# Moving the points at which three token-sum buffers change hands, are folded, loaded and stored

## The chip, the cores and the metric

One core of a Trainium2 chip runs the whole program. The metric is device time in microseconds (us). Shorter names: PE is the matrix engine, DVE the vector engine, ACT the scalar engine, POOL the engine that issues the indirect transfers, SP the engine that issues most of the plain transfers. A transfer moves over 16 DMA engines, whichever engine issued it.

## The reference

Sixteen images of 128 channels and 28x28 pixels pass a convolution block, and their 12544 pixels, as tokens, then pass a mixture of eight experts in which each expert picks its 1024 best tokens. The change touches only how the experts' outputs are added up and written back:

```python
logits = x_flat @ Wr
probs = jax.nn.softmax(logits, axis=0)
vals, idx = jax.lax.top_k(probs.T, C)          # C = 1024 tokens for each of 8 experts
selected = x_flat[idx]
h = jax.nn.gelu(jnp.einsum('ecd,edf->ecf', selected, W1) + b1[:, None, :], approximate=False)
out_e = jnp.einsum('ecf,efd->ecd', h, W2) + b2[:, None, :]
weighted = vals[..., None] * out_e
output = jnp.zeros_like(x_flat).at[idx.reshape(-1)].add(weighted.reshape(-1, Dd))
...
t = t + ffn(layernorm(t));  x = from_tokens(t)  # back to channels by pixels
```

## The kernel before

Everything is ordered by hand: each engine has one program, and semaphores tie them. Experts are numbered 0 to 7 in the code. The convolution and the choice of tokens come first; the experts begin near 240 us and the change lies from 320 us on.

**One expert** on PE is `hidden` for two halves of 512 tokens (4 matmuls each, L936), the turning of the next expert's picked tokens (`turn_picked`, L907), and `down` for two halves (32 matmuls each listed as 16 pairs, L948). ACT does the gelu. DVE adds the bias (`bias_out`, L1437) and multiplies by the gate (`weigh`, L1445) into one of two buffers `y_rows[e % 2]`, so `weigh` of expert e waits until the scatter of expert e - 2 has landed. POOL gathers the tokens of the experts to come in blocks of 128 (`gather`, L472, 8 blocks for an expert) and scatters an expert's result into a sum in DRAM, 8 blocks for an expert. The last expert, `last_expert`, does its two halves one behind the other, so that its first half is scattered while the second is computed.

**Three sum buffers** in DRAM, `moe_sum`, `moe_sum_mid` and `moe_sum_late`, take turns: `FIRST_OF_SUMS` lists the expert that opens each. The opening expert's scatter writes plainly (L495), the others add (L498; L492 for the last expert). An adding scatter waits until the scatter before it has landed, a writing one does not.

**A fold** takes one image of a finished sum: SP loads it as token rows (`load_sums`, L384), PE turns it to channel rows with 7 transposes (`turn_sums`, L978), DVE adds it in two parts to `x1_all` (`add_sums`, L1452). `moe_sum` is folded behind experts 3, 4 and 5 (`FOLDS_BEHIND`), `moe_sum_mid` around the last expert's second half (`MID_FOLDS` ahead of it, the others after). SP issues the loads of a sum once its scatters have landed. PE waits at the end of each group for DVE's folds, since the fold uses PSUM that the next expert needs.

**The end.** `moe_sum_late` is loaded image by image as the last expert's blocks land: `load_late` waits for the turning of that image's middle sum and for as many landed blocks as a number in `need` says, which SP reads from memory. ACT counts landed blocks. PE turns the image (L1033), DVE adds it to `x1_all` into one of four buffers `o_img` (L1521), and the image is stored. SP stores images 0 to 7, in turn with its loads of images 8 to 15, ACT stores images 8 to 15.

```python
for img in range(B):
    load_late(img)
    if img >= B - STORED_BY_SP:
        stored = img - (B - STORED_BY_SP)
        sp.wait_ge(s_fa, stored + 1)
        sp.dma_start(out_d[:, ds(stored, 1), :], o_img[stored % ENDS]).then_inc(...)
```

## Time and profile before

| | us |
|---|---|
| median of 3 runs (470.76 to 477.99) | 471.27 |
| the profiled execution's own time | 471.32 |
| its span in the trace | 469.5 |
| the last expert's last block, issue to landing | 435.26 to 441.40 |
| first output store issued | 440.40 |

Time of day in the trace counts from the span's start; the profiled execution spent 1.8 us outside the span and stands 0.05 us above the median, so a difference of spans is taken as a difference of times. A row of the timeline gives start, duration, engine, line, what is written from what, how many instructions were merged, and in brackets how long the engine sat idle before it and what released it.

### The profile page before, as it was taken

What the parts mean: (1) busy time and instruction counts of PE and PEld (TensorE: products, weight loads), DVE (VectorE), ACT (ScalarE), POOL (GpSimd) and SP (SyncE); (2) the same over time, 40 slices, a digit from 0 to 9 for tenths busy, and PEclk for the clock granted to TensorE, in tenths of its full rate; (3) what the DMA queues carried; (4) which work ended last, traced back from release to release, by engine and by line L of the source; (5) the groups of instructions that cost most, each with busy time, mean ns of one, the idle gap of its engine ahead of it and who ended that gap; (6) DMA issues with size and microseconds to landing.
All of it is one profiled execution on the core that took longest, in us unless ns stands there. A gap on an engine that the chain in (4) does not pass through costs nothing. (4 is left out here: it accounts for less than half of the span.)

```text
span 469.5 us, 8092 instructions
## 1 busy us (share of the span) xinstructions
PE 359.3 (77%) x2577; PEld 249.3 (53%) x2577; DVE 329.2 (70%) x1086; ACT 257.1 (55%) x528; POOL 157.2 (33%) x152
## 2 busy tenths in 40 slices
PE   2778998999999879301148799996998989778752
PEld 2435655666556657200113568766484847637642
DVE  3478788898999886788887697776486342335744
ACT  3469898899998873566701665752343433520000
POOL 4000000000000000010037777787778887766100
PEclk9989999999999995555555999998799989979955
DMA  4456577767676644899902232357986449969897
GB/s 110 128 143 194 159 237 255 227 225 229 201 240 235 194 147 140 261 390 328 320 23 54 54 100 78 76 80 165 296 240 124 86 41 267 290 111 216 260 370 292
DMA packets 42323, 89.07 MB, mean 190 GB/s; under 512 B 7568, under 2 KB 18992, under 8 KB 42288
## 3 DMA queue, kind: packets, MB, share of 16 engines
q1 hardware_dynamic: 32224, 76.62, 51.3%
q0 software_dynamic: 8576, 8.72, 11.0%
q10 hardware_dynamic: 1488, 3.30, 1.8%
q8 instruction: 18, 0.29, 0.3%
q14 instruction: 17, 0.14, 0.1%
HBM read 41.45 MB, written 36.81 MB: 167 GB/s over the span
## 5 line engine op out<-in xcount | busy, mean ns | idle before, releaser
L776 PE MATMUL psC<-x_pad,tap_diag 64*64 64x392 f32 x384 | 68.2, 501 | 8.9 <-issue 5.1
L776 PE MATMUL psC<-hid,tap_turned 64*64 64x392 f32 x384 | 68.2, 501 | 0.0
L503 POOL TENSOR_TENSOR logits_T<-top,logits_T 112x896 f32<-112x896 f32 x1 | 1.7, 1682 | 197.7 <-ACT top L660 197.7
L948 PE MATMUL psC<-w,hid 128*128 128x128 f32 x448 | 52.8, 277 | 1.8 <-ACT hid L702 1.7
L948 PEld LDWEIGHTS psC<-w,hid 128*128 128x128 f32 x448 | 51.0, 192 | 3.9 <-ACT hid L702 3.0
L702 ACT ACTIVATE hid<-psB,b_T 128x512 f32<-128x512 f32 x32 | 21.9, 687 | 53.9 <-PE psB L936 53.9
L776 PEld LDWEIGHTS psC<-x_pad,tap_diag 64*64 64x64 f32 x384 | 28.0, 135 | 37.6 <-issue 28.7
L472 POOL DMA_INDIRECT picked<-token_rows,slot_idx x32 | 31.3, 979 | 45.7 <-issue 44.8
L936 PE MATMUL psB<-picked_T,w 128*128 128x512 f32 x64 | 37.6, 719 | 6.5 <-DVE x_all L1452 3.3
L580 ACT ACTIVATE ln_tok<-psA,sm 112x128 f32<-112x128 f32 x112 | 40.9, 477 | 0.9 <-DVE sm L1089 0.9
L1437 DVE TENSOR_TENSOR y_sum<-psC,b_rows 128x512 f32<-128x512 f32 x14 | 9.6, 688 | 39.3 <-PE psC L948 39.3
L1097 DVE SCALAR_TENSOR_TENSOR work<-x_pad,taps_w,work 128x784 f32<-128x784 f32 x32 | 33.1, 1035 | 1.1
L806 PE MATMUL psB<-work,pw_masked 128*128 128x392 f32 x64 | 26.5, 539 | 5.3 <-DVE pw_masked L1203 2.7
L936 PE MATMUL psC<-picked_T,w 128*128 128x512 f32 x64 | 30.5, 599 | 0.0
L873 PE MATMUL psA<-sign_sum,half_same 128*128 128x4 f16 x16 | 3.0, 187 | 35.2 <-ACT x_in L640 34.2
L1097 DVE SCALAR_TENSOR_TENSOR work<-x_pad,taps_w,psC 128x392 f32<-128x392 f32 x32 | 18.5, 619 | 14.4 <-PE psC L776 14.4
L1046 DVE BATCH_NORM_STATS2 st<-psA 112x6 f32<-112x128 f32 x112 | 23.7, 282 | 7.0 <-PE psA L815 6.9
L603 ACT ACTIVATE work<-psB,fold 128x392 f32<-128x392 f32 x32 | 21.0, 678 | 12.3 <-PE psB L806 12.3
L672 ACT ACTIVATE picked_T<-psA 128x512 f32<-128x512 f32 x16 | 8.8, 594 | 33.0 <-PE psA L907 33.0
L498 POOL DMA_INDIRECT moe_sum_mid<-y_rows,slot_idx x16 | 25.1, 1568 | 4.9 <-issue 4.9
L776 PEld LDWEIGHTS psC<-hid,tap_turned 64*64 64x64 f32 x384 | 25.8, 135 | 0.0
L1293 DVE TENSOR_SCALAR_CACHE_REDUCE work<-dist,cand 128x784 bf16<-128x784 f32 (+1 forms) x31 | 24.6, 829 | 1.1 <-DVE cand L1311 0.7
(280 smaller groups left out, 873.3 us busy)
## 6 DMA issues: line engine op xcount, KB each, us to landing
token_rows<-rows SPq DMA_DIRECT2D x16, 422.6 KB, 4.9
x_in<-in_x_dram SPq DMA_DIRECT2D x16, 392.0 KB, 3.4
x_res<-in_x_dram SPq DMA_DIRECT2D x16, 392.0 KB, 4.0
moe_sum<-hid SPq DMA_DIRECT2D x16, 392.0 KB, 4.5
x_all<-work SPq DMA_DIRECT2D x16, 392.0 KB, 3.0
moe_sum_mid<-hid SPq DMA_DIRECT2D x16, 392.0 KB, 5.7
moe_sum_late<-hid SPq DMA_DIRECT2D x16, 392.0 KB, 4.8
w<-in_L_ffn_W_dram SPq DMA_DIRECT2D x16, 256.0 KB, 3.1
```

The source lines that it names most:

```text
L472: nc.gpsimd.indirect_dma_start(out=picked_in[k][:, b, :], out_offset=None, in_=rows_dram, in_offset=bass.IndirectOffsetOnAxis(ap=slot_idx[ ...
L498: nc.gpsimd.indirect_dma_start(out=sums, out_offset=at, in_=y_rows[:, q, b, :], in_offset=None, compute_op=ALU.add).then_inc(s_sca[q], 16)
L580: ins = nc.scalar.activation(ln_tok[:, q1, t * C:(t + 1) * C], ln_tiles[:, t, :], ACT.Identity, bias=ln_sm[:, 6, t:t + 1], scale=ln_sm[:, ...
L603: nc.scalar.activation(act2[:, q3, h * HALF:(h + 1) * HALF], psB[:, h, 0:HALF], ACT.Relu, bias=fold[:, 9:10], scale=fold[:, 5:6]).then_inc ...
L702: nc.scalar.activation(hid[:, f, h * HS:(h + 1) * HS], hidden_bank[f], ACT.Gelu, bias=b1_T[:, ds(e * FT + f, 1)]).then_inc(s_gelu, 1)
L776: ins = nc.tensor.matmul(psC[col * HC:col * HC + HC, half, 0:HALF].rearrange("c (h w) -> c h w", w=W), weights[of, n, :], lines[of, q, dy: ...
L806: nc.tensor.matmul(psB[:, h, 0:HALF], pw_masked[:, q, :], act1[:, q, h * HALF:(h + 1) * HALF], start=True, stop=True).then_inc(s_pw, 1)
L936: nc.tensor.matmul(hidden_bank[f], w1[:, q, f * 128:(f + 1) * 128], picked_T[:, h * HS:(h + 1) * HS], start=True, stop=True).then_inc(s_l1, 1)
L948: ins = nc.tensor.matmul((psA if first else psC)[:, h, b * C:(b + 1) * C], hid[:, f, lo:lo + 128], w2[:, q, f * C:(f + 1) * C], start=(f = ...
L1046: ins = nc.vector.bn_stats(st[:, t, :], ln_tiles[:, t, :])
L1097: return nc.vector.scalar_tensor_tensor(o, x_pad_v[:, q, y0 + dy:y0 + dy + lines, dx:dx + W], taps_w[:, PE_TAPS + n:PE_TAPS + n + 1], acc, ...
L1293: return nc.vector.tensor_scalar(junk[:, column, 0:n], dist[:, 0:n], value.bitcast(F32), -offset, ALU.is_lt, ALU.add, accum_out=cnt[:, col ...
```

## The change

The sums are cut at experts 0 to 2, 3 to 5 and 6 to 7, where they were cut at 0 to 1, 2 to 4 and 5 to 7. The first is folded behind experts 4, 5 and 6 (5, 7 and 4 images), where it was behind 3, 4 and 5 (4, 6 and 6). Of the middle sum, one image is folded between `hidden` and `down` of the last expert's first half, two behind that `down`, and 13 behind the second half, where it was 6 and 10. SP only loads at the end; ACT stores all 16 images.

```diff
-FIRST_OF_SUMS = (0, 2, 5)
-FOLDS_BEHIND = {3: range(0, 4), 4: range(4, 10), 5: range(10, B)}
-MID_FOLDS = 6
-STORED_BY_SP = 8
+FIRST_OF_SUMS = (0, 3, 6)
+FOLDS_BEHIND = {4: range(0, 5), 5: range(5, 12), 6: range(12, B)}
+FOLDS_AT_LAST = (range(0, 1), range(1, 3), range(3, B))
+STORES_AMONG_BLOCKS = 1
@@ SP: loads of the first and the middle sum, the end
-                if e == 5:
-                    sp.wait_ge(s_sca[0], 16 * SB)
+                if e == 6:
+                    sp.wait_ge(s_sca[0], 2 * 16 * SB)
                     sp.wait_ge(s_sca[1], 16 * SB)
...
             sp.wait_ge(s_sca[0], 3 * 16 * SB)
-            sp.wait_ge(s_sca[1], 2 * 16 * SB)
+            sp.wait_ge(s_sca[1], 3 * 16 * SB)
...
                 load_late(img)
-                if img >= B - STORED_BY_SP:
-                    stored = img - (B - STORED_BY_SP)
-                    sp.wait_ge(s_fa, stored + 1)
-                    sp.dma_start(out_d[:, ds(stored, 1), :], o_img[stored % ENDS]).then_inc(s_fo[stored % ENDS], 16)
@@ POOL: scatter
-                if e in (3, 6):
+                if e in (4, 7):
                     pool.wait_ge(s_sca[q], e // 2 * (16 * SB))
@@ ACT: the end
+            def store_image(img):
+                act.wait_ge(s_fa, img + 1)
+                act.dma_start(out_d[:, ds(img, 1), :], o_img[img % ENDS]).then_inc(s_fo[img % ENDS], 16)
             for b in range(SB):
                 act.wait_ge(s_blk[b], 16)
                 act.sem_inc(s_landed, 1)
-            for img in range(STORED_BY_SP, B):
-                act.wait_ge(s_fa, img + 1)
-                act.dma_start(out_d[:, ds(img, 1), :], o_img[img % ENDS]).then_inc(s_fo[img % ENDS], 16)
+                if b >= SB - STORES_AMONG_BLOCKS:
+                    store_image(b - (SB - STORES_AMONG_BLOCKS))
+            for img in range(STORES_AMONG_BLOCKS, B):
+                store_image(img)
@@ PE: expert, last_expert
                 if e in FOLDS_BEHIND:
-                    pe.wait_ge(s_ptc, (e + 1) * 2 + 2)
+                    pe.wait_ge(s_ptc, (e + 1) * 2 + (2 if another else 0))
...
                 hidden(e, q, 0, {})
+                for img in FOLDS_AT_LAST[0]:
+                    turn_sums(1, img)
                 pe.wait_ge(s_w2[q], use * 16 + 16)
                 down(e, q, 0)
-                for img in range(MID_FOLDS):
+                for img in FOLDS_AT_LAST[1]:
                     turn_sums(1, img)
                 turn_picked(e, 1)
-                pe.wait_ge(s_fk, 2 * (B + MID_FOLDS))
+                pe.wait_ge(s_fk, 2 * (B + FOLDS_AT_LAST[1].stop))
                 hidden(e, q, 1, {})
                 down(e, q, 1)
-                for img in range(MID_FOLDS, B):
+                for img in FOLDS_AT_LAST[2]:
                     turn_sums(1, img)
@@ DVE: last_expert
+                    if h == 0:
+                        for img in FOLDS_AT_LAST[0]:
+                            add_sums(1, img)
                     bias_out(e, h)
                     weigh(e, q, use, h)
-                    for img in (range(MID_FOLDS), range(MID_FOLDS, B))[h]:
-                        add_sums(1, img)
                     if h == 0:
                         norm_picked(e, 1)
+                    for img in FOLDS_AT_LAST[1 + h]:
+                        add_sums(1, img)
```

POOL's transfers from the scatter of expert 2 to the end. L472 is a gather, L495 a writing scatter, L498 and L492 an adding one. First the order before:

```order
L495 DMA moe_sum_mid<-y_rows,slot_idx 12544x128 x8
L472 DMA x_in<-token_rows,slot_idx 128x138 x8
L498 DMA moe_sum_mid<-y_rows,slot_idx 12544x128 x8
L472 DMA x_res<-token_rows,slot_idx 128x138 x4
L498 DMA moe_sum_mid<-y_rows,slot_idx 12544x128 x8
L495 DMA moe_sum_late<-y_rows,slot_idx 12544x128 x8
L472 DMA x_res<-token_rows,slot_idx 128x138 x4
L498 DMA moe_sum_late<-y_rows,slot_idx 12544x128 x8
L492 DMA moe_sum_late<-y_rows,slot_idx 12544x128 x8
```

And now, on the same engine and in the same stretch (L468 is the gather, L491 writes, L494 and L488 add):

```order
L494 DMA moe_sum<-y_rows,slot_idx 12544x128 x8
L468 DMA x_in<-token_rows,slot_idx 128x138 x8
L491 DMA moe_sum_mid<-y_rows,slot_idx 12544x128 x8
L468 DMA x_res<-token_rows,slot_idx 128x138 x4
L494 DMA moe_sum_mid<-y_rows,slot_idx 12544x128 x16
L468 DMA x_res<-token_rows,slot_idx 128x138 x4
L491 DMA moe_sum_late<-y_rows,slot_idx 12544x128 x8
L488 DMA moe_sum_late<-y_rows,slot_idx 12544x128 x8
```

The scatter of expert 2 adds and that of 3 writes; the scatters of 4 and 5 are both adding ones and stand back to back, and that of 6 writes.

PE in the last expert, from the turning of its first half's tokens to its second half. L907 turns picked tokens, L936 is `hidden`, L948 `down`, L978 the folds of the middle sum. Before:

```order
L907 MATMUL psA<-ident,x_res 128x128 x4
L936 MATMUL psB<-picked_T,w 128x512 x2
L936 MATMUL psC<-picked_T,w 128x512 x2
L948 MATMUL psA<-w,hid 128x128 x16
L978 MATMUL psD<-ident,ln_tok 128x112 x7
L978 MATMUL psB<-ident,ln_tok 128x112 x7
L978 MATMUL psD<-ident,x_pad 128x112 x7
L978 MATMUL psB<-ident,x_pad 128x112 x7
L978 MATMUL psD<-ident,work 128x112 x7
L978 MATMUL psB<-ident,work 128x112 x7
L907 MATMUL psA<-ident,x_res 128x128 x4
```

Now, with the folds of the first sum behind expert 6 ahead of it (L979 folds, L908, L937 and L949 as above):

```order
L979 MATMUL psB<-ident,rows 128x112 x7
L979 MATMUL psA<-ident,logits 128x112 x7
L979 MATMUL psB<-ident,logits_T 128x112 x7
L979 MATMUL psA<-ident,s_cmp 128x112 x7
L908 MATMUL psA<-ident,x_res 128x128 x4
L937 MATMUL psB<-picked_T,w 128x512 x2
L937 MATMUL psC<-picked_T,w 128x512 x2
L979 MATMUL psD<-ident,ln_tok 128x112 x7
L949 MATMUL psA<-w,hid 128x128 x16
L979 MATMUL psB<-ident,ln_tok 128x112 x7
L979 MATMUL psD<-ident,x_pad 128x112 x7
L908 MATMUL psA<-ident,x_res 128x128 x4
```

Four folds of the first sum now stand ahead of the last expert, one fold ahead of its first `down`, and two, not six, ahead of the turning of its second half.

SP at the end, from the load of the late sum's image 8. L416 reads the number of blocks needed, L384 loads, L424 stores. Before:

```order
L416 TENSOR_LOAD need
L416 ISA x2
L384 DMA work<-moe_sum_late 112x896
L424 DMA out_dram<-hid 128x784
L416 TENSOR_LOAD need
L416 ISA x2
L384 DMA work<-moe_sum_late 112x896
L424 DMA out_dram<-hid 128x784
```

Now:

```order
L416 TENSOR_LOAD need
L416 ISA x2
L384 DMA work<-moe_sum_late 112x896
L416 TENSOR_LOAD need
L416 ISA x2
L384 DMA work<-moe_sum_late 112x896
```

No store, and so no wait for DVE's output, stands between two loads any more.

## Rows read from the trace of the kernel before

**Rows 1.** The page's first line.

```profile
span 469.5 us, 8092 instructions
```

**Rows 2.** Chain that ended last, one piece: start, us, what.

```profile
435.26 6.14 DMA moe_sum_late<-y_rows,slot_idx
```

**Rows 3.** Timeline of POOL, first or last block of a gather or scatter.

```profile
317.98 1.55 POOL L498 DMA_INDIRECT moe_sum<-y_rows,slot_idx  x1 [0.30 <-issue]
...
330.23 0.99 POOL L495 DMA_INDIRECT moe_sum_mid<-y_rows,slot_idx  x1 [0.30 <-issue]
...
350.83 1.63 POOL L498 DMA_INDIRECT moe_sum_mid<-y_rows,slot_idx  x1 [0.30 <-issue]
...
365.84 1.02 POOL L472 DMA_INDIRECT x_res<-token_rows,slot_idx  x1 [0.30 <-issue]
...
370.95 1.62 POOL L498 DMA_INDIRECT moe_sum_mid<-y_rows,slot_idx  x1 [0.31 <-issue]
...
395.19 0.96 POOL L495 DMA_INDIRECT moe_sum_late<-y_rows,slot_idx  x1 [0.30 <-issue]
...
402.59 1.64 POOL L498 DMA_INDIRECT moe_sum_late<-y_rows,slot_idx  x1 [1.38 <-DMA moe_sum_late<-y_rows,slot_idx]
...
419.87 1.55 POOL L492 DMA_INDIRECT moe_sum_late<-y_rows,slot_idx  x1 [2.55 <-DMA moe_sum_late<-y_rows,slot_idx]
...
429.67 1.55 POOL L492 DMA_INDIRECT moe_sum_late<-y_rows,slot_idx  x1 [2.65 <-DVE y_rows L1445]
```

**Rows 4.** Timeline of PE, 325 to 417 us.

```profile
325.25 1.45 PE L978 MATMUL psB<-ident,ln_tok 112*128 112x112 f32 x7 [3.27 <-DMA ln_tok<-moe_sum]
...
332.32 3.60 PE L936 MATMUL psB<-picked_T,w 128*128 128x512 f32 x4 [0.60 <-DVE x_all L1452]
...
357.40 1.98 PE L936 MATMUL psB<-picked_T,w 128*128 128x512 f32 x4 [1.35 <-DVE x_all L1452]
...
372.39 0.84 PE L978 MATMUL psB<-ident,work 112*128 112x112 f32 x7
...
379.80 3.64 PE L936 MATMUL psB<-picked_T,w 128*128 128x512 f32 x4 [1.35 <-DVE x_all L1452]
...
397.24 1.98 PE L936 MATMUL psB<-picked_T,w 128*128 128x512 f32 x4 [0.69 <-ACT picked_T L672]
...
416.89 3.75 PE L936 MATMUL psB<-picked_T,w 128*128 128x512 f32 x4 [0.73 <-issue]
```

**Rows 5.** Timeline of DVE, 321 to 466 us.

```profile
321.39 0.69 DVE L1445 TENSOR_TENSOR y_rows<-y_sum,gate 128x512 f32<-128x512 f32 x1 [2.71 <-DMA moe_sum<-y_rows,slot_idx]
...
407.40 0.69 DVE L1445 TENSOR_TENSOR y_rows<-y_sum,gate 128x512 f32<-128x512 f32 x1
...
413.69 1.30 DVE L1410 TENSOR_SCALAR x_res<-x_res 128x128 f32<-128x128 f32 x4
...
428.10 0.69 DVE L1445 TENSOR_TENSOR y_rows<-y_sum,gate 128x512 f32<-128x512 f32 x1
...
437.23 1.02 DVE L1452 TENSOR_TENSOR x_all<-psB,x_all 128x448 f32<-128x448 f32 x2
...
460.35 1.04 DVE L1521 TENSOR_TENSOR hid<-psC,x_all 128x448 f32<-128x448 f32 x2 [1.75 <-PE psA L1033]
...
465.02 1.04 DVE L1521 TENSOR_TENSOR hid<-psC,x_all 128x448 f32<-128x448 f32 x2
```

**Rows 6.** Timeline of SP's queue, first late loads and first store.

```profile
423.19 1.22 SPq L384 DMA_DIRECT2D ln_tok<-moe_sum_late  x2
...
440.40 0.36 SPq L424 DMA_DIRECT2D out_dram<-hid  x1
```

**Rows 7.** DMA issues: KB of one, median us from issue to landing.

```profile
out_dram<-hid SPq DMA_DIRECT2D x8, 392.0 KB, 5.9
out_dram<-hid ACTq DMA_DIRECT2D x8, 392.0 KB, 3.6
```

**Rows 8.** Windows, 440.4 us to the end: length, busy by engine, PEclk, DMA share, GB/s.

```profile
440.40:469.50 29.10, 14.75 (x93) 11.99 (x91) 14.94 (x30) 0.00 (x0) 0.00 (x0) 0.63 0.88 318
```

## The prediction

> **What bounds the kernel now.** The chain of waits comes first: its last link before the output stores is the landing of the last expert's last scatter block, issued at 435.26 and landed 6.14 us later, at 441.40 [rows 2], in a span of 469.5 us [rows 1]. From there I go back on POOL's timeline [rows 3]. The reader is to see that POOL has no real pause from the scatter of expert 2 at 330.23 to 402.59: the idle time ahead of its blocks is 0.30 us of issue. Behind that it waits three times: 1.38 us and 2.55 us for a landing, and 2.65 us at 429.67 for DVE's second half of the last expert. So two chains run close together, POOL's transfers and PE's experts with the folds between them, and at 429.67 PE and DVE are the later. The timelines of PE and DVE give the pace of that second chain [rows 4, 5]; the window on the end shows 318 GB/s over 29.1 us from the first store on [rows 6, 8], with the output stores taking 5.9 us where SP's loads run beside them and 3.6 us where they don't [rows 7].
>
> **Prices.** Eight adding blocks take 365.84 - 350.83 = 15.0 us of POOL; four gathers 370.95 - 365.84 = 5.1; eight gathers and eight writes 350.83 - 330.23 = 20.6, so eight writes 10.4 [rows 3]. The number of each kind is the same after the change, only their places move. A landing is seen at 317.98 to 321.39 = 3.4 us from the start of the last block to the waiter's start, and, beside the loads of the middle sum, at 395.19 to 402.59 = 7.4 us [rows 3, 5]. Ten folds end at 437.23 + 1.02 = 438.25 and begin behind the row at 428.10 + 0.69: 0.945 us for each where data are there [rows 5]. Where the loads were only just issued, four folds took 332.32 - 325.25 = 7.07 us, 1.77 each [rows 4].
>
> **Folds behind experts 4, 5 and 6.** The scatter of expert 2 now adds: from 330.23 its last block begins 13.1 us later (seven eighths of 15.0), at 343.3, and lands at 346.7, where the scatter that the first loads waited for was seen landed at 321.39. That is 25.3 us later. DVE's `weigh` of expert 4 waits for the same landing (the other use of its buffer), as that of expert 3 did at 321.39, and behind it on DVE's queue stand the slot search of expert 7, the bias of the second half and the folds. PE has skipped the folds behind expert 3 but can't use it: its first fold moves from 325.25 to 350.6. Four folds later it is 357.6, the fifth makes it 359.4, against the 357.40 at which expert 5 began: 2.0 us late. PE has then been idle for some 9 us, and the row behind the earlier case of this kind shows the first four `hidden` matmuls at 3.60 us where the same four took 1.98 at 357.40 [rows 4], another 1.6. At the end of expert 5 the chain is 3.6 us late, 376.0 for 372.39. Seven folds for six add 0.9: expert 6 begins at 379.80 + 4.5 = 384.3. Behind it come four folds that were not there. Six cost 379.80 - 372.39 = 7.4 from the end of `down`, so four cost 7.4 - 1.9 = 5.5, and the last expert's `hidden` begins at 397.24 + 4.5 + 5.5 = 407.2, 10.0 us late. Whether that `hidden` starts at the slow pace (1.6 more) the rows don't decide: after folds it did at 379.80 and did not at 357.40; I take no charge, and keep 1.6 for the high end.
>
> **The last expert.** Its single early fold needs the middle sum's first image. On POOL the scatter of expert 4 begins at 370.95 as before, its last block lands at 387.5, and only then may the scatter of 5 begin, which now adds: it ends at 402.5 and lands at 404.0. SP issues the loads, and the first is there some 3.9 us later (321.39 to 325.25 before), at 407.9. PE wants it at 407.2 + 3.7 = 410.9, the end of `hidden`, and would stand still anyway for the gelu until 407.2 + 5.5. So that fold costs nothing, with 3.0 us to spare; if the load comes later than that, each us is paid. `weigh` of the first half moves from 407.40 to 417.4. Behind it come now the norm of the second half's tokens (1.30 us), and the two folds run beside their turning; before, six folds stood between. `hidden` of the second half followed the norm by 416.89 - 414.99 = 1.9 us, so it begins at 417.4 + 0.7 + 1.3 + 1.9 = 421.3: of the 10.0 us only 4.4 are left. That carries to the second half's scatter: 429.67 + 4.4 = 434.1.
>
> POOL would allow it: four gathers 402.5 to 407.6, the scatter of 6 as writes to 418.0 with its last block begun at 416.7, landed at 420.1 or, beside the middle loads as at 395.19, at 424.1; four blocks of the first half (7.5) end at 427.6 or 431.6. PE's chain decides by 2.5 us or more. The gathers of the second half's tokens, issued 6 us later than before, are needed at 418.1; at the 7.4 us of a slowed landing they are there at 415.
>
> **The end.** The last block lands at 441.40 + 4.4 = 445.8. Thirteen folds for ten add 3 x 0.945 = 2.8: the last ends at 438.25 + 4.4 + 2.8 = 445.5, and the first store goes at 440.40 + 7.2 = 447.6. It is issued by ACT behind the last block's landing, which is earlier. What is left then is a tail that took 29.1 us. Late loads began at 423.19, will begin some 4 us later, and are no longer held behind stores. From below: sixteen outputs, the first four at 0.945 us, twelve at the pace of the last outputs, (465.02 - 460.35) / 4 = 1.17, and 3.6 us for the last landing: 2.8 + 14.0 + 3.6 = 20.4. From above: the 29.1 us of before, if nothing is won. I take the bytes: sixteen stores and two loads still open (between none and the seven that were open before) of 392 KB, 7.2 MB, at the 318 GB/s of the window: 22.7 us. 447.6 + 22.7 = 470.3, 0.8 us more than the span before. With the 1.8 us around the span, and the profiled run standing at the median, that is 472.1 us: no change, since a difference of 2% (9.4 us) is about what this measurement tells from none.
>
> **A rule against it.** The rows say that stores took 5.9 us beside loads and 3.6 us without, and that the end moved 318 GB/s [rows 7, 8]. The Trainium skill, "DMA: Bandwidth & Descriptors", section "Issuing engines are not separate DMA queues", states that transfers from all issuing engines run on the same 16 DMA engines, so that issuing from several saves only issue time. By it a queue of its own for the stores gives nothing unless loads also move to an earlier, emptier stretch, and the tail would stay near 29.1.
>
> **The rivals.** First, the tail is bound by bytes and keeps its length, 29.1 us, because the late loads also start 4 us later and meet scatter traffic until the last block lands. 447.6 + 29.1 = 476.7, 478.5 us. It makes the kernel slower than before from a tail of 469.5 - 447.6 = 21.9 us on. For it: the DMA share was 0.88 in that window [rows 8]. Against it: SP's loads of images 9 to 15 stood behind stores before, so part of the tail was waiting and not bytes. Second, PE's chain is shorter than I make it, because the loads of the first sum come faster than 1.77 us an image or PE gets its pace back at once. Then POOL decides, 2.5 us earlier: 445.1 + 20.4 = 465.5, 467.3 us. For it: POOL's scatters keep 2.5 us of room even in the slow case; against it: four images did wait for their loads in the row at 325.25. A gain over 2% would need the first store before 440, which POOL's transfers forbid in both cases.
>
> **How the numbers follow.** I give 0.55 to the forecast, 0.2 to the tail that keeps its length, 0.2 to the shorter chain, 0.05 to what I don't see. Low: 467.3 less the slow start of the last `hidden` (3.75 for 1.98, 1.8) gives 465. High: 478.5 with a slow `hidden` in the first half (1.6) gives 480. Slower by over 2% is 480.7: I give 0.11, from the first rival with a further delay; faster, below 461.8, 0.08; the rest, 0.81, lies within.
>
> **What would show it.** In the new profile: a pause of POOL of 1.5 to 3 us ahead of the scatter of 5; PE idle for some 9 us ahead of the folds behind expert 4 and expert 5 starting near 359; the last `hidden` of the first half near 407 and of the second near 421; the first store at 446 to 449 on ACT; the tail from it 20 to 24 us, with SP issuing its late loads in one run before 450. The prediction is wrong if PE begins expert 5 before 355, if the early fold waits for its load, or if the stores keep near 6 us each.

## The result, and the profile after

The changed kernel took 479.02 us in the median of 6 runs (476.13 to 481.93), the kernel before 473.23 us in the 6 runs beside them (470.76 to 477.99). The ratio is 1.0189, with a 95% interval of 1.0153 to 1.0225: 1.9% slower, where the forecast was no change at 472.1 us. The time lies within the range that was given, 465 to 480, and near the price of the first rival, 478.5. Executions of one kernel fall into a faster and a slower state; ratios here and below are of the faster one alone, medians are of all runs.

The page's first line of the changed kernel, beside 469.5 before [rows 1]:

```profile
span 480.1 us, 8092 instructions
```

The profiled execution (481.93 us) is the longest of the six, and its experts came late: the scatter of expert 2, for which both kernels have done the same work, starts 2.3 us later than before. So below, "from the scatter of 2" means from that row, at 332.54 here and at 330.23 before [rows 3]. On this scale the end went from 139.3 to 147.6 us, 8.3 us in one trace of each kernel where the medians differ by 5.8, so what is read from one trace may be 2 or 3 us off. Timeline of POOL, the changed kernel, first or last block of a scatter, or first after a wait:

```profile
332.54 1.62 POOL L494 DMA_INDIRECT moe_sum<-y_rows,slot_idx  x1 [0.30 <-issue]
...
391.41 1.55 POOL L494 DMA_INDIRECT moe_sum_mid<-y_rows,slot_idx  x1 [2.52 <-DMA moe_sum_mid<-y_rows,slot_idx]
...
420.32 0.96 POOL L491 DMA_INDIRECT moe_sum_late<-y_rows,slot_idx  x1 [0.30 <-issue]
427.73 1.62 POOL L488 DMA_INDIRECT moe_sum_late<-y_rows,slot_idx  x1 [6.45 <-DMA moe_sum_late<-y_rows,slot_idx]
...
437.76 1.55 POOL L488 DMA_INDIRECT moe_sum_late<-y_rows,slot_idx  x1 [2.79 <-DVE y_rows L1448]
```

The pause ahead of the scatter of 5 (2.52 us) is the one foretold. The pause ahead of the last expert's first half is 6.45 us for 2.55 [rows 3], and the second half waits for DVE as before, 2.79 for 2.65 us, so PE and DVE are still the later chain. Timeline of PE, the same kernel:

```profile
352.98 1.54 PE L979 MATMUL psB<-ident,ln_tok 112*128 112x112 f32 x7 [8.76 <-DMA ln_tok<-moe_sum]
...
362.00 3.78 PE L937 MATMUL psB<-picked_T,w 128*128 128x512 f32 x4 [0.60 <-DVE x_all L1455]
365.57 3.20 PE L937 MATMUL psC<-picked_T,w 128*128 128x512 f32 x4
...
370.32 1.88 PE L937 MATMUL psC<-picked_T,w 128*128 128x512 f32 x4
...
388.41 3.53 PE L937 MATMUL psB<-picked_T,w 128*128 128x512 f32 x4 [1.35 <-DVE x_all L1455]
...
411.43 1.98 PE L937 MATMUL psB<-picked_T,w 128*128 128x512 f32 x4 [0.69 <-ACT picked_T L668]
...
425.26 2.84 PE L937 MATMUL psB<-picked_T,w 128*128 128x512 f32 x4 [1.24 <-DVE x_all L1455]
```

PE is idle for 8.76 us, where the prediction said some 9, and expert 5 starts 29.5 us after the scatter of 2, where it said 29.2. The slow clock then lasts longer than before: the second four `hidden` matmuls are slow too, 3.20 us where the same take 1.88 at 370.32. Before, only the first four behind the pause were slow [rows 4]; the next four, timeline of PE, the kernel before:

```profile
335.75 1.88 PE L936 MATMUL psC<-picked_T,w 128*128 128x512 f32 x4
```

The end, in the chain that ended last and on the queues of SP and ACT (start, us, what):

```profile
436.88 12.31 DVE x_all L1455 x26
...
450.26 3.89 DVE hid L1527 x8
454.18 11.55 DMA out_dram<-hid
...
470.82 4.73 DMA out_dram<-hid
```

```profile
435.56 1.24 SPq L384 DMA_DIRECT2D ln_tok<-moe_sum_late  x2
437.40 1.21 SPq L384 DMA_DIRECT2D x_pad<-moe_sum_late  x2
439.21 11.44 SPq L384 DMA_DIRECT2D work<-moe_sum_late  x7
451.26 1.21 SPq L384 DMA_DIRECT2D rows<-moe_sum_late  x2
...
455.80 0.30 SPq L384 DMA_DIRECT2D s_cmp<-moe_sum_late  x1
451.34 25.72 ACTq L740 DMA_DIRECT2D out_dram<-hid  x16
```

The first store goes at 451.34, 118.8 us from the scatter of 2, against 110.2 before. The 13 last folds take 12.31 us, 0.947 each, where 0.945 was assumed. But the tail is not the 22.7 us of the forecast. Its window, beside 29.10 us and 318 GB/s before [rows 8], and two parts of it:

```profile
451.30:480.10 28.80, 13.68 (x93) 12.11 (x91) 14.96 (x31) 0.00 (x0) 0.00 (x0) 0.72 0.90 324
451.30:459.60 8.30, 3.77 (x37) 3.33 (x35) 2.84 (x7) 0.00 (x0) 0.00 (x0) 0.84 1.03 306
459.60:466.00 6.40, 4.13 (x20) 3.53 (x21) 3.30 (x7) 0.00 (x0) 0.00 (x0) 0.50 1.03 412
```

324 GB/s over 28.8 us are 9.33 MB: sixteen stores of 0.40 MB and 7.2 loads. Before it was 318 x 29.1 = 9.25 MB, 7.0 loads. What the loads wait for has changed, though. SP's waits, before from 415 to 455 us and after from 427 to 457 us (line, releaser, us in total, times, longest):

```profile
SPq L384 <- ACTq L744: 8.0, 5, 3.3
SPq L424 <- DVE hid L1521: 5.4, 2, 5.1
```

```profile
SPq L384 <- ACTq L744: 13.8, 4, 7.8
```

Before, the loads waited 5.4 us behind the first stores and 8.0 us for landed blocks of the last expert (which ACT counts at L744). After, the wait behind stores is gone and the one for landed blocks is 5.8 us longer. Even so the loads go sooner behind the first store than before: 12 of 16 are issued ahead of it where it was 9, and the last one follows it by 4.5 us (455.80 for 451.34) where it was 11.9. SP's queue before, from the third late load on, first store at 440.40 [rows 6]:

```profile
426.05 1.21 SPq L384 DMA_DIRECT2D x_pad<-moe_sum_late  x2
429.54 5.77 SPq L384 DMA_DIRECT2D work<-moe_sum_late  x5
...
452.33 0.30 SPq L384 DMA_DIRECT2D s_cmp<-moe_sum_late  x1
```

What did not come sooner is their landing. DMA issues (KB, median us from issue to landing), before and after:

```profile
work<-moe_sum_late SPq DMA_DIRECT2D x7, 392.0 KB, 4.7
```

```profile
work<-moe_sum_late SPq DMA_DIRECT2D x7, 392.0 KB, 6.4
```

The windows from about the first late load to the first store, before and after:

```profile
423.00:440.40 17.40, 14.17 (x124) 12.52 (x125) 11.91 (x25) 0.39 (x1) 9.65 (x7) 1.00 0.96 236
```

```profile
435.00:451.30 16.30, 13.25 (x116) 11.05 (x115) 14.72 (x31) 0.00 (x0) 6.24 (x4) 1.00 1.00 240
```

The DMA engines were 0.96 busy there before and are 1.00 busy now, and they move about as much, 4.1 and 3.9 MB. So loads that are issued earlier stay open, and some seven of them are left for the tail, as before.

### The profile page after: what moved, and what is told of

The parts are those of the page before. It is cut to its first block, busy times and chain, and to the rows that moved or that the text cites. A ratio compares the mean times of both kernels' runs of the same rounds, so it can differ in the third digit from the quotient of the medians.

```text
span 480.1 us, 8092 instructions
## 1 busy us (share of the span) xinstructions
PE 359.6 (75%) x2577; PEld 248.1 (52%) x2577; DVE 330.3 (69%) x1086; ACT 257.2 (54%) x528; POOL 156.8 (33%) x152
## 4 chain that ended last, share of the span: by engine, by line
PE 27%; DVE 18%; ACT 17%; issue 13%; POOL 13%; DMA 8%; SPq 2%; ACTq 0%; DVEq 0%; POOLq 0%
PE psC L777 6%; DVE x_all L1455 5%; ACT ln_tok L576 5%; POOL moe_sum L494 4%; POOL picked L468 4%; PE psC L949 4%; PE psB L807 4%; DMA out_dram<-hid 3%; PE psB L937 3%; PE psC L937 2%; DVE hid L1527 2%; DMA work<-moe_sum 2%; PE psB L795 2%; ACT x_in L636 2%; DVE work L1100 2%
## 5 line engine op out<-in xcount | busy, mean ns | idle before, releaser
L777 PE MATMUL psC<-x_pad,tap_diag 64*64 64x392 f32 x384 | 71.8, 522 | 9.6 <-issue 5.6
L777 PE MATMUL psC<-hid,tap_turned 64*64 64x392 f32 x384 | 71.7, 522 | 0.0
L949 PE MATMUL psC<-w,hid 128*128 128x128 f32 x448 | 52.8, 277 | 1.8 <-ACT hid L698 1.7
L949 PEld LDWEIGHTS psC<-w,hid 128*128 128x128 f32 x448 | 51.0, 192 | 4.0 <-ACT hid L698 3.0
L777 PEld LDWEIGHTS psC<-x_pad,tap_diag 64*64 64x64 f32 x384 | 29.2, 141 | 40.6 <-issue 33.9
L468 POOL DMA_INDIRECT picked<-token_rows,slot_idx x32 | 31.4, 980 | 45.7 <-issue 44.5
L937 PE MATMUL psB<-picked_T,w 128*128 128x512 f32 x64 | 34.9, 673 | 5.7 <-DVE x_all L1455 3.2
L937 PE MATMUL psC<-picked_T,w 128*128 128x512 f32 x64 | 32.8, 636 | 1.9 <-DVE y_sum L1440 1.9
L494 POOL DMA_INDIRECT moe_sum_mid<-y_rows,slot_idx x16 | 25.0, 1562 | 8.0 <-issue 4.3
L599 ACT ACTIVATE work<-psB,fold 128x392 f32<-128x392 f32 x32 | 21.0, 678 | 11.9 <-PE psB L807 11.9
L698 ACT ACTIVATE hid<-psC,b_T 128x512 f32<-128x512 f32 x32 | 21.9, 688 | 10.1 <-PE psC L937 10.1
L494 POOL DMA_INDIRECT moe_sum<-y_rows,slot_idx x16 | 25.4, 1590 | 4.9 <-issue 4.9
```

Source lines behind the costliest of these rows:

```text
L468: nc.gpsimd.indirect_dma_start(out=picked_in[k][:, b, :], out_offset=None, in_=rows_dram, in_offset=bass.IndirectOffsetOnAxis(ap=slot_idx[ ...
L494: nc.gpsimd.indirect_dma_start(out=sums, out_offset=at, in_=y_rows[:, q, b, :], in_offset=None, compute_op=ALU.add).then_inc(s_sca[q], 16)
L599: nc.scalar.activation(act2[:, q3, h * HALF:(h + 1) * HALF], psB[:, h, 0:HALF], ACT.Relu, bias=fold[:, 9:10], scale=fold[:, 5:6]).then_inc ...
L698: nc.scalar.activation(hid[:, f, h * HS:(h + 1) * HS], hidden_bank[f], ACT.Gelu, bias=b1_T[:, ds(e * FT + f, 1)]).then_inc(s_gelu, 1)
L777: ins = nc.tensor.matmul(psC[col * HC:col * HC + HC, half, 0:HALF].rearrange("c (h w) -> c h w", w=W), weights[of, n, :], lines[of, q, dy: ...
L937: nc.tensor.matmul(hidden_bank[f], w1[:, q, f * 128:(f + 1) * 128], picked_T[:, h * HS:(h + 1) * HS], start=True, stop=True).then_inc(s_l1, 1)
```

## The experiments

Four theories stood at the start. **Theory 1**: the end is bound by bytes, loads that move later fill the DMA engines beside the last scatters and stay open into the tail. **Theory 2**: PE's first folds wait for the scatter of 2, and that delay travels to the end. **Theory 3**: the stores in a queue of their own hurt, since they then compete with the loads. **Theory 4**: the tail is the round trip of the four output buffers, since an output waits for the store of four images earlier. "Tail" is the time from the first output store to the end of the span.

| kernel | median us | ratio, 95% interval | first store, from scatter of 2 | tail us | GB/s |
|---|---|---|---|---|---|
| e1 | 472.42 | 0.9991, 0.9936 to 1.0047 | 110.8 | 28.1 | 317 |
| e2 | 470.77 | 0.9977, 0.9933 to 1.0021 | 108.4 | 30.7 | 309 |
| e3 | 485.90 | 1.0304, 1.0197 to 1.0410 | 119.9 | 27.8 | 333 |
| e4 | 478.86 | 1.0146, 1.0055 to 1.0237 | 116.0 | 30.4 | 315 |
| e5 | 475.27 | 1.0120, 1.0051 to 1.0190 | 119.0 | 25.8 | 323 |
| e6 | 478.70 | 1.0188, 1.0116 to 1.0259 | 115.7 | 29.9 | 338 |
| e7 | 484.81 | 1.0288, 1.0194 to 1.0382 | | | |
| e8 | 470.09 | 0.9994, 0.9948 to 1.0040 | 111.0 | 27.9 | 322 |
| e9 | 478.40 | 1.0165, 1.0103 to 1.0228 | 119.7 | 22.4 | 343 |
| e10 | 470.48 | 0.9981, 0.9937 to 1.0025 | 103.4 | 32.0 | 343 |
| e11 | 476.16 | 1.0140, 1.0032 to 1.0248 | 119.0 | 25.7 | 233 |
| e12 | 469.12 | 0.9945, 0.9894 to 0.9996 | 108.2 | 24.4 | 263 |
| e13 | 480.05 | 1.0143, 1.0083 to 1.0203 | 118.9 | 26.5 | 336 |
| e14 | 471.89 | 0.9953, 0.9907 to 1.0000 | 108.3 | 28.7 | 330 |
| e15 | 470.25 | 0.9923, 0.9887 to 0.9959 | 103.2 | 33.0 | 333 |
| e16 | 472.56 | 0.9996, 0.9951 to 1.0041 | 119.0 | 20.7 | 283 |
| e17 | 466.03 | 0.9922, 0.9851 to 0.9993 | 108.8 | 24.2 | 249 |

The ratios are against the kernel before, run beside each. The last three columns are of one profiled execution, which can lie some us off the median (e12 5.6 us below it, e10 3.0 below, e2 3.2 above). Those of e7 and e16 are not among the runs that their ratios count; e7's is left out, and of e16's, 2.4 us above its median, only the first store and the window of the tail are used.

**e1, the stores alone moved (kernel before).**

```diff
-STORED_BY_SP = 8
+STORED_BY_SP = 0
...
```

> The kernel before with one edit: ACT stores all 16 images, SP only loads. Theory 1 (the end is bound by bytes, and the change's loss comes from transfers that were moved later): no loss from the queue, the late loads of images 9 to 15 run earlier, tail from the first store 26 to 29 us, time 0 to 3 us less than before. Theory 3 (a queue of its own makes the stores compete with the loads, packet by packet): the first stores take 8 us and more, the tail is 31 us or more, time 2 to 5 us more.

No change. SP is free of the stores, and issued its last late load at 445.81, 1.9 us behind the first store (in the kernel before 11.9 us, 452.33 for 440.40). Yet the first store takes some 8 us to land, as Theory 3 had it, the fifth output waits 7.94 us for it, and the tail is 1.0 us shorter, with no gain in time. Timeline of DVE, e1:

```profile
452.19 1.04 DVE L1517 TENSOR_TENSOR hid<-psB,x_all 128x448 f32<-128x448 f32 x2 [7.94 <-DMA out_dram<-hid]
```

The loads that went earlier stand, as I read it, in front of the store on the DMA engines (see e8).

**e2, the split 1, 2 and 13 of the middle folds alone (kernel before).**

```diff
-MID_FOLDS = 6
+FOLDS_AT_LAST = (range(0, 1), range(1, 3), range(3, B))
...
```

> The kernel before with one edit: the middle sum is folded 1, 2 and 13 instead of 6 and 10, all cuts as before. All theories: hidden of the last half starts 3 to 5.5 us earlier (411 to 414), POOL's wait for DVE at the last half goes to 0 and POOL decides, 2 to 2.5 us earlier; 13 folds end at 438 to 440 for 438.25. Theory 1: the first store comes at 439 to 442, time 0 to 2 us less than before. If the 13 folds alone made the loss, time 2 to 3 us more.

No change that the interval shows. `hidden` of the second half starts at 414.19, and POOL no longer waits for DVE ahead of its scatter: with the old cuts POOL's own transfers are the next thing late, so PE's lead is worth little.

**e3, the first cut alone (kernel before).**

```diff
-FIRST_OF_SUMS = (0, 2, 5)
-FOLDS_BEHIND = {3: range(0, 4), 4: range(4, 10), 5: range(10, B)}
+FIRST_OF_SUMS = (0, 3, 5)
+FOLDS_BEHIND = {4: range(0, 5), 5: range(5, 12), 6: range(12, B)}
...
```

> The kernel before with the first sum made of experts 0 to 2 and folded behind 4 to 6, the middle sum 3 and 4, the late one 5 to 7, 6 and 10 folds at the end and stores as before. Theory 2 (the wait of the first folds for the scatter of 2 is what costs): PE idle 8 to 9 us ahead of the folds behind expert 4, expert 5 begins 2 us late, the last expert's hidden 11 to 12 us late, the last half's scatter 10 to 12 us late, time 7 to 11 us more than before. Theory 1 (the loads of the middle sum 20 us later are what costs): those loads start near 388 as before, the tail becomes shorter, time 2 to 6 us more.

The slowest of all, level with e7; its ratio rests on two runs, and its profiled execution, 478.81 us, is the shortest of its four, so its rows show the cause rather than its whole size. Timelines of PE and POOL, e3:

```profile
349.84 1.54 PE L978 MATMUL psB<-ident,ln_tok 112*128 112x112 f32 x7 [7.40 <-DMA ln_tok<-moe_sum]
```

```profile
438.43 1.55 POOL L492 DMA_INDIRECT moe_sum_late<-y_rows,slot_idx  x1 [11.58 <-DVE y_rows L1445]
```

PE waits 7.40 us for the first loads, four folds stand ahead of the last expert, and POOL, whose other scatters are within some 1 us of where they were, waits 11.58 us for the last half. That is Theory 2 without late middle loads. The wait is only part of it: of the 10.4 us by which the last expert's first `hidden` comes late on the scale from the scatter of 2, 5.5 are the four folds ahead of it (399.75 to 405.27).

**e4, the middle cut alone (kernel before).**

```diff
-FIRST_OF_SUMS = (0, 2, 5)
+FIRST_OF_SUMS = (0, 2, 6)
...
```

> The kernel before with the middle sum made of experts 2 to 5 and the late one of 6 and 7, all else as before. The loads of the middle sum wait for the scatter of 5. Theory 1: they start near 404, DMA share 1.0 from there to 430, the scatter of 6 is seen landed 7 us and more after its last block began, six folds ahead of the last half wait for loads, late loads begin 6 to 12 us later, time 5 to 10 us more than before. Theory 2: PE's experts up to the last one's first half are on time, and the time is within 3 us of before.

Slower by another way. The middle sum's loads go at 404.70, for 387.82 before, so they run beside the last scatters. Windows of 21 us around them, e4 and then before, and POOL in e4:

```profile
404.00:425.00 21.00, 15.01 (x82) 11.51 (x83) 8.77 (x19) 4.80 (x7) 11.31 (x13) 0.73 0.97 282
```

```profile
404.00:425.00 21.00, 15.72 (x92) 10.94 (x91) 8.29 (x19) 6.41 (x9) 15.71 (x11) 0.84 0.75 161
```

```profile
424.69 1.62 POOL L492 DMA_INDIRECT moe_sum_late<-y_rows,slot_idx  x1 [6.34 <-DMA moe_sum_late<-y_rows,slot_idx]
```

The DMA share rises from 0.75 to 0.97, and POOL waits 6.34 us for a landing that cost 2.55 before [rows 3]. That is Theory 1's half of the delay.

**e5, half the bytes of the middle loads (changed kernel; the other half of the middle sum is left out).**

```diff
-                load_sums(mid_t, img)
+                half = sums_in[img][0:P // 2, :]
+                sp.dma_start(half.rearrange("p (t c) -> p t c", c=C), mid_t[0:P // 2, ds(img, 1), :, :]...)
```

> The changed kernel, but each load of the middle sum takes 56 of the 112 rows of partitions, half the bytes; the other half of each fold is left out of the result. Theory 1 (transfers moved later fill the DMA engines from the middle loads to the end): the scatter of 6 is seen landed in 4 to 5 us instead of 7.4, late loads begin 3 to 7 us earlier than in the changed kernel, fewer of them are open at the first store, tail 24 to 27 us for 28.8, time 4 to 9 us less than the changed kernel, 470 to 475. Theory 2 (PE's chain behind the scatter of 2 sets the end): the chain is the same up to the last half, time within 2 us of the changed kernel, 477 to 481.

By the medians 3.7 us of the change's cost went, by the ratios 0.7%, and the two intervals overlap. In the trace 3.0 us of it are in the tail, and the first late load goes 3.5 us earlier on the scale from the scatter of 2. The landing of the scatter of 6 did not get faster (8.4 us from its last block to the next scatter). That of the last expert's first block did: the first late load follows its start by 3.4 us (429.23 for 425.86), where it was 7.8 in the changed kernel (435.56 for 427.73) and 3.3 before (423.19 for 419.87). So what slows a landing is only in part these bytes.

**e6, the stores put back (changed kernel).**

```diff
-STORES_AMONG_BLOCKS = 1
+STORED_BY_SP = 8
...
```

> The changed kernel with the stores as before: SP stores images 0 to 7 in turn with its loads of 8 to 15, ACT the rest. Theory 1: the tail is bound by bytes either way, 28 to 31 us from the first store, time within 2 us of the changed kernel. Theory 3 (the queue of the stores is to blame): time 3 to 6 us less than the changed kernel.

The same time as the changed kernel. With e1 and e8 this leaves Theory 3 nothing beyond the intervals, some 0.5% to 0.7% either way.

**e7, both cuts, nothing else (kernel before with both edits of e3 and e4).**

> The kernel before with both cuts moved and the first sum folded behind 4 to 6, but with 6 and 10 folds of the middle sum and the stores as before. Both theories on the cuts: slower than the changed kernel by what three folds ahead instead of six give back, since PE's chain is the later one there: 3 to 6 us more than the changed kernel, 482 to 486. If the fold order gives nothing back, 479.

A ratio of 1.0288 against 1.0188 of e6, which differs from it only in the split 1, 2 and 13. So the split gives back some 1.0%, 5 us, with the new cuts, where PE is late, though in e2 it gave nothing; the two intervals overlap. The time is no more than that of e3, so the costs of the two cuts (3.0% and 1.5% alone) don't add.

**e8, the old cuts and everything else new (edits of e1 and e2 together).**

> The kernel before with the two parts that are not cuts: 1, 2 and 13 folds, and all stores on ACT. Theory 1: first store waits for the last block, which lands 1.5 to 2.5 us earlier than before, tail 28 to 30 us, time 0 to 3 us less than before, 469 to 472. If the two parts hurt together, 474 or more.

No change. The loss lies in the cuts. The run also shows what a free queue is worth. SP's last late load, the tail's window and the DMA issue, e8:

```profile
442.34 0.30 SPq L384 DMA_DIRECT2D s_cmp<-moe_sum_late  x1
```

```profile
440.56:468.50 27.94, 12.09 (x80) 10.52 (x77) 13.74 (x28) 0.00 (x0) 0.00 (x0) 0.70 0.89 322
```

```profile
work<-moe_sum_late SPq DMA_DIRECT2D x7, 392.0 KB, 6.9
```

No load waits behind a store, the wait for landed blocks is about as long as before (8.7 us for 8.0), and 14 of 16 late loads are issued ahead of the first store at 440.56. The tail is still 27.9 us and moves 9.0 MB, sixteen stores and 6.4 loads: these loads take 6.9 us to land for 4.7 before. So neither of SP's two waits is what keeps the tail long.

**e9, half the bytes of the late loads of images 9 to 15 (changed kernel; the other half of these is left out).**

```diff
-                load_sums(late_t, img)
+                if img < 9:
+                    load_sums(late_t, img)
+                else:
+                    half = sums_in[img][0:P // 2, :]
+                    sp.dma_start(half.rearrange(...), late_t[0:P // 2, ds(img, 1), :, :]...)
```

> The changed kernel, but the loads of the late sum for images 9 to 15 take half the bytes; the other half is left out of the result. Theory 1 (the tail is the bytes still open at the first store, at 309 to 338 GB/s): 7 x 0.2 MB less, tail 24 to 25.5 us for 28.8, time 3 to 5 us less than the changed kernel. Theory 4 (the tail is bound by the round trip of the four output buffers, whatever else moves): tail 28 to 29 us, time as the changed kernel.

The tail of its trace fell to 22.4 us, close to the forecast's 22.7, and the fifth output waits 1.89 us for the first store and not 5.47. But its median moved only 0.6 us, with its chain 0.9 us later. The trace speaks for open loads as the tail's length, with the stores whole and the four buffers in place; the time does not confirm it, and why it moved so little is open.

**e10, eight outputs among the last folds (kernel before).** PE turns a late image between two folds of the middle sum, in two regions of PSUM, and SP stores from its load of image 6 on.

```diff
+                    if img - MID_FOLDS - 2 >= 0:
+                        turn_out(img - MID_FOLDS - 2)
```

> The kernel before, with the first eight output images turned and added among the last ten folds of the middle sum (two PSUM regions for them instead of four), and SP storing images 0 to 9, the first behind the load of image 6. Theory 1: the first store comes 5 to 9 us earlier, near 432 to 436, the bytes are the same, and only what the DMA engines stood idle in the tail before (0.12 of 29 us) can be won: 1 to 4 us less than before, 467 to 470. Theory 4: the outputs start earlier and the round trips with them, 5 to 8 us less. If the outputs hold up the folds and these the late loads, 0 to 4 us more than before.

The first store goes 6.8 us earlier, and the time stays within its interval: the tail is 2.9 us longer with 11.0 MB open.

**e11 and e12, half of each output left out (changed kernel, kernel before).**

```diff
-act.dma_start(out_d[:, ds(img, 1), :], o_img[img % ENDS])
+act.dma_start(out_d[0:C // 2, ds(img, 1), :], o_img[img % ENDS][0:C // 2])
```

> The changed kernel, with each of the 16 output stores moving only the first half of the channels (the other half of the output is left out). Every wait, fold and load is as in the changed kernel. Theory 1 (the end is bound by the bytes that are open when the first store goes): 9.33 MB less 16 x 0.20 MB leave 6.1 MB, 18.9 us at 324 GB/s, so the tail falls from 28.8 us to 19 to 21 us (20.4 us is the pace of the outputs themselves), and the time falls by 8 to 10 us, to 469 to 471, about that of the kernel before. Rival (the end is bound by the round trip of the late loads or of the four output buffers, whatever they move): the tail stays at 26 us or more and the time at 476 or more.

> The kernel before, with each of the 16 output stores moving only the first half of the channels (the other half of the output is left out). Theory 1 (bytes): 9.25 MB less 3.2 MB leave 6.0 MB, 19 us at 318 GB/s, so the tail falls from 29.1 us to 19 to 22 us and the time to 462 to 465. The distance to the changed kernel with half stores stays at the 7 to 9 us by which the first store goes later. Rival (stores between loads on SP's queue are what makes the tail of the kernel before long, so that the kernel before has waiting in its tail that the changed one has not): its tail falls less than that of the changed kernel, to 24 us or more.

3.2 MB less, and the tails fall by 3.1 and 4.7 us only, not by the 8 to 10 of Theory 1. In e11 the outputs stand still again. Timeline of DVE, e11:

```profile
455.63 1.04 DVE L1527 TENSOR_TENSOR hid<-psB,x_all 128x448 f32<-128x448 f32 x2 [5.75 <-DMA out_dram<-hid]
```

So in e11, with fewer bytes, the four buffers hold the tail: the fifth output waits for the first store, which went out behind the open loads.

**e13 and e14, outputs in place (changed kernel, kernel before).** Each output is written over its image in `x1_all` and stored from there, so no output waits for a store.

```diff
-        o_img = [hid[:, k:k + 1, 0:HW] for k in range(ENDS)]
+        o_img = [x1_all[:, k * HW:(k + 1) * HW].rearrange("c (o n) -> c o n", o=1) for k in range(B)]
...
-                if img >= ENDS:
-                    dve.wait_ge(s_fo[k], img // ENDS * 16)
...
```

> The changed kernel, but DVE writes each output over its image in x1_all and the store reads it there, so that no output waits for the store four images earlier. Theory 4 (the tail is set by the round trip of the four output buffers): the 10.4 us that DVE waits for stores in the tail go (5.47, three of about 1.03 and 1.86), and the tail falls from 28.8 to what its 9.33 MB take at the fastest rate seen there, 386 to 412 GB/s, 23 to 25 us; the time falls to 473 to 475. Theory 1 (bytes at a rate that no buffer changes): the tail stays at 28 to 29 us and the time at 478 to 480, with the waits only moved from DVE's outputs to the landing of the stores.

> The kernel before with outputs in place, as in the run beside it. Theory 4: its seven waits of DVE for stores, 9.0 us, go, and 9.25 MB at 386 GB/s take 24 us for 29.1, so the time falls to 466 to 468, a ratio of 0.99. Theory 1: the tail stays near 29 us, ratio 1.00.

Theory 4 fails as the only limit. Timeline of DVE, DMA issue and the tail's window, e13:

```profile
451.56 1.03 DVE L1525 TENSOR_TENSOR x_all<-psB,x_all 128x448 f32<-128x448 f32 x2
...
467.27 1.04 DVE L1525 TENSOR_TENSOR x_all<-psC,x_all 128x448 f32<-128x448 f32 x2 [0.74 <-PE psC L1036]
```

```profile
out_dram<-x_all ACTq DMA_DIRECT2D x16, 392.0 KB, 13.0
```

```profile
452.23:478.70 26.47, 9.79 (x63) 7.46 (x61) 11.32 (x23) 0.00 (x0) 0.00 (x0) 0.66 0.94 336
```

The fifth output follows the fourth at once, the last is done at 468.3 for 476.7 in the changed kernel, and the stores then wait on the DMA engines: 13.0 us from issue to landing for 4.7 in the changed kernel. The time is that of the changed kernel within the intervals, though the tail of this trace is 2.3 us shorter. e14's interval touches one, and its tail is 0.4 us shorter than that of the kernel before.

**e15, e10 with outputs in place.**

> The kernel before with eight outputs among the last folds of the middle sum, and now in place. Theory 4: its seven waits of 0.4 to 1.7 us go and the tail of 32.0 us falls to 28 to 29 (10.96 MB at 386 GB/s), the time to 466 to 468. Theory 1: the tail stays at 31 to 32 us, the time near 470, ratio 1.00.

The best of the kernels that write the whole output: 0.8% faster than the kernel before, the interval clear of one, though its tail is 33.0 us.

**e16 and e17, both at once: outputs in place and half of each left out (changed kernel, kernel before).**

> The changed kernel with outputs in place and half of each output left out: neither the bytes of the stores nor the four buffers hold the tail as before. Two limits side by side (bytes, some 26 to 29 us, and the round trip of the buffers, some 24 to 26 us, so that taking one away shows the other): the tail falls to what 6.0 MB take at 320 GB/s, 18 to 21 us, and the time to 468 to 472, well below both single edits (476.2 with half stores, 480.1 in place). A third limit that neither touches (the landing of the late loads): the tail stays at 24 us or more, the time at 474 to 477.

> The kernel before with outputs in place and half of each output left out. Two limits: the tail falls from 24.4 us (half stores alone) and 28.7 us (in place alone) to 19 to 21 us, the time to 462 to 466. A third limit: the tail stays near 24 us, the time near 469.

Windows of the tail, e11, then e16:

```profile
448.05:473.70 25.65, 11.50 (x83) 10.16 (x81) 13.74 (x28) 0.00 (x0) 0.00 (x0) 0.77 0.84 233
```

```profile
452.07:472.80 20.73, 11.80 (x68) 9.05 (x66) 12.26 (x25) 0.00 (x0) 0.00 (x0) 0.66 0.95 283
```

In the changed kernel both edits give what neither gives alone: a tail of 20.7 us for 26.5 (in place) and 25.7 (half stores), and a ratio of 0.9996 for 1.0143 and 1.0140. There are two limits side by side, bytes and the four buffers. In the kernel before the tail stays at 24.2 us, as the expectation had it for a third limit, though the time fell to 466.03. There SP still takes its loads in turn with its stores, a pair in 1.5 to 1.9 us and once in 3.4, and the last late load goes at 454.01, 12.8 us behind the first store; this turn-taking, which the changed kernel doesn't have, can hold it. That was not tested by itself. The delay ahead of the first store stays, whatever the tail: 118.9 to 119.0 us from the scatter of 2 in the changed kernel (e11, e13, e16) for 108.2 to 108.8 in the kernel before (e12, e14, e17).

## Why the prediction was wrong

**The two chains, and which is later**: right. PE's pause, the pause of POOL ahead of the scatter of 5, the early fold that costs nothing behind the gelu, DVE as the last releaser of POOL all stand in the trace. The first store is 8.6 us later for a forecast of 7.2.

**The slow clock, "another 1.6"**: mis-sized. The eight first `hidden` matmuls of expert 5 took 3.78 + 3.20 = 6.98 us, where 1.98 + 1.88 would be full pace, so 3.1: 1.5 us more than charged, and the first store missed by 1.4. The windows of the changed kernel, PEclk third from the end:

```profile
353.00:362.00 9.00, 7.54 (x36) 6.09 (x36) 6.68 (x14) 0.00 (x0) 6.87 (x8) 0.50 1.04 282
362.00:368.60 6.60, 6.60 (x8) 2.75 (x9) 2.42 (x9) 2.06 (x3) 5.08 (x6) 0.53 1.04 324
368.60:373.00 4.40, 4.40 (x18) 2.43 (x17) 0.00 (x0) 3.41 (x6) 3.49 (x4) 1.00 1.04 324
```

**The last expert**: right in its sum. From the scatter of 2, `hidden` of its second half was forecast at 91.1 and came at 92.7, the same 1.6 us late as the clock.

**The tail, "sixteen stores and two loads still open"**: this is the step that failed. The bytes of seven loads were open, and the tail took 28.8 us and not 22.7: 6.1 of the 7.5 us by which the end missed on the scale from the scatter of 2 (147.6 for 140.1). The two was chosen "between none and the seven" without a row for it, on the reading that the loads stood open since they waited behind stores. That wait went, and 12 loads for 9 were issued ahead of the first store, but the DMA engines, 0.96 busy in that stretch before and 1.00 after, moved about 4 MB ahead of the store in both kernels, and what was issued sooner took longer to land. e1 and e8 show the same with the old cuts, where the middle loads are not late: a free load queue left 6.2 and 6.4 loads in tails of 28.1 and 27.9 us.

Nor did the late loads start "some 4 us later" while the first store moved by more. The first went 103.0 us from the scatter of 2, for 97 forecast and 93.0 before: 10.0 us later, with the first store only 8.6 later. Of the 10.0, 5.6 are POOL's wait for the scatter of 6 and what stands ahead of it (427.73 for 419.87 on that scale), 4.5 the landing of the last expert's first block, 7.8 us for 3.3, beside the middle loads. e4, where the middle cut alone was moved, shows this by itself: 6.34 us of wait, then 6.8 us to the first late load (431.50 for 424.69). The longer wait for landed blocks is a sign of it; e8, where that wait did not grow and the tail was as long, speaks against it as the tail's cause.

**The first rival** named the outcome and the reason that holds best, late loads that "meet scatter traffic". That its price, 478.5 us, was only 0.5 us low is partly luck: it stood 7.2 us above 471.3, where the medians differ by 5.8 and the two traces by 8.3 from the scatter of 2 on. A queue for the stores alone gave 0.9991 (e1) and 0.9994 (e8), and taking it away again 1.0188 for 1.0189 (e6). By that, the runs agree with the rule of the Trainium skill, "DMA: Bandwidth & Descriptors", section "Issuing engines are not separate DMA queues". What the rival lacked is that bytes are one of two limits: with 6.0 MB left by half stores the four buffers still held the tail at 25.7 us (e11). The forecast's price for fewer open loads was sound in the one trace that has it: with 7.7 MB left by half loads the tail was 22.4 us (e9).

**The second rival**, a shorter PE chain with POOL deciding, does not hold: POOL waited 2.79 us for DVE.

What stays open: why the scatter of 6 lands late when the middle loads are halved (e5), why e9's time hardly moved, and what holds e17's tail.

## What to carry to other kernels

When a queue's wait is removed, ask whether the DMA engines have room in the stretch that the transfers move into, and not only when the queue lets them go: here the loads no longer stood behind stores, and since the engines were 0.96 busy ahead of the first store already, as many were left open. Moving transfers later is no free move, since they land beside what the end waits for. Where a tail can be held by bytes and by buffers, one edit that eases one of them proves nothing; take both away before calling either the limit.

## What the runs showed of the hardware

A scatter block took longer to land where the DMA engines were busier: the eight blocks of the last expert took a median of 7.4 us from issue after (DMA share 1.02 from 427.73 to 451.3) and 5.8 us before (0.85 from 419.87 to 440.4). That the load beside it is the whole reason is not shown (e5). Late loads that were issued sooner, as seen from the first store, took longer to land: the seven into `work` took a median of 6.9 us in e8 and 6.4 in the changed kernel, for 4.7 before. Over whole tails with loads and stores mixed the rate was 309 to 343 GB/s in every kernel with full outputs; within them it was 306 GB/s in the first 8.3 us of the changed kernel's tail and 412 GB/s from 459.6 to 466.0, where SP had issued all its loads. At a granted clock of 0.50 to 0.53, the lower of the two levels (1.2 GHz), PE ran 15.6 us of folds and `hidden` behind its idle 8.76 us, before it rose to 1.00.
